# Second expert stage: weights per block from DRAM into a ring, in place of a resident copy

## The chip, the cores and the metric

The kernel runs on one core of one Trainium2 chip. The metric is the device time of the program in microseconds, of which several runs are taken. The engines are PE (matrix products), DVE, ACT and POOL (elementwise work; POOL also starts indirect DMAs) and SP (which only starts DMAs). Each has its own stream of instructions; they meet through semaphores.

## What is computed

The input x has 128 graphs of 64 nodes with 128 features, 8192 tokens in all. Four parts follow each other, each adding to x what it makes of the normalised x:

```python
x = x + gated_graph(layernorm(x), adj)      # 3 GRU layers
x = x + experts_1(layernorm(x))             # 8 experts, top 2, relu
x = x + relational(layernorm(x), adj)       # 40 relations, two directions
x = x + experts_2(layernorm(x))             # 8 experts, top 2, gelu
```

The last of them, which the change is about, computes all experts for all tokens and takes two per token:

```python
top_p, top_idx = jax.lax.top_k(probs, 2)
weights = top_p / top_p.sum(axis=-1, keepdims=True)
xe = xn[None, :, :] * ln_g[:, None, :] + ln_b[:, None, :]
h = gelu(jnp.einsum('end,edh->enh', xe, W1) + b1[:, None, :])   # h: 512 wide
y = jnp.einsum('enh,ehd->end', h, W2) + b2[:, None, :]
```

The kernel computes only the two chosen experts of each token.

## The kernel before

**Stages.** The program runs setup, first_norm, gated_graph, experts "1", relational, experts "2" and combine one behind the other; a barrier of all engines stands between them. The function `experts` is used twice, with m = 0 for the first and m = 1 for the second. In the trace the tiles of the second have names that begin with e2, those of the first with e1.

**Routing and blocks.** Each token is sent twice, once for each of its experts, from the tile ROWS in SBUF into a DRAM array `slots`, where the rows of one expert stand together. These sends are POOL's indirect DMAs (L570), 256 in a stage; most are issued in the stage before, and the last 32 at the start and in the first iterations of the expert stage, four per iteration. The slots are worked off in 39 blocks of 512 rows. A block belongs to one expert, which depends on the data: a table `owner` gives it, `start_row` the block's first row. Eight "tail" DMAs (L1259, one per expert, in the iterations b = 3 to 10) fill up the last rows of each expert.

**One block.** SP loads the block's rows transposed into xT (L1246 reads the row number from the table, L1247 is the DMA) and its labels (L1253). PE computes the up product, 4 chunks of 128 hidden rows with 3 matmuls each (the weights are kept as a high and a low f16 half, L358 to L360). ACT applies the bias and the activation (L1356, L1361), DVE splits the result (L1374). PE opens the output with the b2 rows (L1317, 2 matmuls) and computes the down product with 32 matmuls (L1323, L1325). DVE weighs and sums the two halves (L1409, L1411, L1415), and POOL scatters the 512 rows to `results` with 4 indirect DMAs (L1293). PE's order is the up product of block b+1, then the down product of block b. All buffers are rings of three (RING = 3). Blocks 0 to 2 and 33 to 38 are written out, blocks 3 to 32 run in a hardware loop of 5 turns of 6 blocks (L59, L1234).

**Where the weights are.** W1 and W2 in SBUF hold both halves of all 8 experts, 2 MB each. Since the owner of a block is data, PE reads it into a register (L1304, once before the up and once before the down product) and addresses the weights with it:

```python
def who(b):
    return pe.value_load(owner[0:1, bass.ds(b, 1)], min_val=0, max_val=E - 1)
passes(pe, HB[c][:, :], lambda s: W1[:, s, bass.ds(e * HID + c * P, P)],
       lambda s: xT[j][:, s, :], True, True).then_inc(h_ps, 1)
```

The second stage's weights are prepared during gated_graph and written to two DRAM arrays, kept[0] and kept[1]. At the start of the relational stage, when the first experts are through, SP loads both back into W1 and W2 (L1558 to L1560), ahead of its other DMAs. Those are four row loads (L1562) and the tiles c_G (L1433), the expert results which DVE adds to X (L1426). At its end SP waits for the two reloads. In combine the results are loaded as d_G by the same line.

## Time and profile before

| | us |
|---|---|
| median of 3 runs | 1657.19 |
| the runs | 1643.72, 1657.19, 1658.66 |
| the profiled execution's own time | 1653.87 |
| its span | 1652.1 |
| experts "1" (from its first xT load) | 604 to 946 |
| relational | 946 to 1267 |
| experts "2", first matmul to last scatter | 1279 to 1605 |
| combine, first load to the end | 1609 to 1652 |

The profile is of one execution. Its rows give a start in us from the span's start, a duration in us, the engine, the line of the kernel and the operation, out<-in by tile names. "q" behind an engine's name (SPq) marks its sequencer, which issues DMAs. In brackets stands how long the engine had been idle and what released it: "issue" means that nothing the profile shows was being waited for, and "remote" that it was a semaphore from another engine whose last visible operation had long ended. PE matmul rows overlap, since the ends are modelled.

### The profile page before, as it was taken

Reading aid. Unit: us, or ns where it says so; the run is one execution under the profiler, and the core shown is the slowest. Engines: PE = TensorE matmul, PEld = TensorE weight load, DVE = VectorE, ACT = ScalarE, POOL = GpSimd, SP = SyncE. Lnnn points to the kernel's source line nnn. Section 1 sums busy time; section 2 is a strip of 40 time slices with the busy share of each in tenths; the row PEclk is TensorE's granted clock in tenths of the full one; section 3 lists DMA queues with packets and bytes.
Section 4 is the critical chain, followed back from the end, with each engine's and each line's share of the span. In section 5 each row is a group of like instructions: output and inputs, shape, how many; then the busy total and the mean of one; then the engine's idle time right before and its main releaser. Section 6 shows DMA issues by size and latency. Waiting matters only on the chain. (4 is left out here: it accounts for less than half of the span.)

```text
span 1652.1 us, 23983 instructions
## 1 busy us (share of the span) xinstructions
PE 970.9 (59%) x6685; PEld 540.3 (33%) x6686; DVE 993.0 (60%) x2486; ACT 745.7 (45%) x1300; POOL 777.8 (47%) x751
## 2 busy tenths in 40 slices
PE   2046758676850625678898334545440767898850
PEld 1023324333330512345554212322220424455530
DVE  5957778878784333456666425565662444676645
ACT  0135556464541533456665324544540534666630
POOL 2322324757546005665666501156665366565650
PEclk8569989898875556889999755555555778999985
DMA  7010010202105342433333141021101334333309
GB/s 191 0 26 1 20 32 24 56 28 62 40 21 161 128 115 66 97 79 73 71 64 70 30 146 39 27 66 60 47 33 51 78 81 93 74 74 65 79 10 304
DMA packets 234271, 114.92 MB, mean 70 GB/s; under 512 B 172816, under 2 KB 218002, under 8 KB 233656
## 3 DMA queue, kind: packets, MB, share of 16 engines
q1 hardware_dynamic: 203400, 69.07, 18.3%
q0 software_dynamic: 18176, 34.14, 6.5%
q10 hardware_dynamic: 12592, 10.49, 2.3%
q8 instruction: 45, 0.74, 0.2%
q14 instruction: 58, 0.48, 0.1%
HBM read 41.76 MB, written 51.08 MB: 56 GB/s over the span
## 5 line engine op out<-in xcount | busy, mean ns | idle before, releaser
L570 POOL DMA_INDIRECT slots<-ROWS,pos x256 | 269.8, 1054 | 159.1 <-POOLq L152 86.3
L1293 POOL DMA_INDIRECT results<-e1ys,e1home x156 | 167.3, 1072 | 129.2 <-DVE e1ys L1415 82.8
L1293 POOL DMA_INDIRECT results<-e2ys,e2home x156 | 169.6, 1087 | 121.1 <-DVE e2ys L1415 75.4
L1356 ACT ACTIVATE e1hf<-psum,VT 128x512 f32<-128x512 f32 x156 | 104.3, 687 | 149.8 <-remote 76.9
L1356 ACT ACTIVATE e2hf<-psum,VT 128x512 f32<-128x512 f32 x156 | 104.1, 688 | 131.6 <-remote 84.4
L1176 POOL TENSOR_TENSOR a_gates<-a_gates,a_state 128x512 f32<-128x512 f32 x48 | 62.8, 1308 | 166.8 <-ACT a_gates L923 165.9
L1323 PE MATMUL psum<-W,e1hs 128*128 x624 | 120.5, 286 | 25.0 <-issue 21.1
L1323 PE MATMUL psum<-W,e2hs 128*128 x624 | 121.5, 285 | 22.7 <-issue 20.2
L1374 DVE SCALAR_TENSOR_TENSOR e1hs<-e1hf,e1hs 128x512 f16<-128x512 f32 x156 | 101.8, 690 | 42.8 <-ACT e1hs L1361 35.7
L1325 PE MATMUL psum<-W,e2hs 128*128 x624 | 114.9, 227 | 16.5 <-issue 16.3
L1325 PE MATMUL psum<-W,e1hs 128*128 x624 | 114.3, 227 | 16.6 <-issue 16.5
L1374 DVE SCALAR_TENSOR_TENSOR e2hs<-e2hf,e2hs 128x512 f16<-128x512 f32 x156 | 101.1, 688 | 36.5 <-ACT e2hs L1361 27.1
L1545 POOL TENSOR_TENSOR c_rs<-c_var,mhalf 128x12 f32<-128x12 f32 (+2 forms) x19 | 37.8, 1990 | 151.8 <-DVE c_var L1802 119.4
L1361 ACT ACTIVATE e2hs<-e2hf 128x512 f16<-128x512 f32 x156 | 94.3, 635 | 0.0
L1361 ACT ACTIVATE e1hs<-e1hf 128x512 f16<-128x512 f32 x156 | 94.2, 634 | 0.0
L358 PE MATMUL psum<-e1xT,W 128*128 128x512 f16 x156 | 61.9, 396 | 40.3 <-DMA e1xT<-slots 31.7
L1409 DVE TENSOR_SCALAR e2both<-psum 128x512 f32<-128x512 f32 x39 | 26.8, 688 | 97.5 <-remote 97.2
L1409 DVE TENSOR_SCALAR e1both<-psum 128x512 f32<-128x512 f32 x39 | 26.8, 688 | 91.9 <-remote 91.2
L1323 PEld LDWEIGHTS psum<-W,e2hs 128*128 128x128 f16 x624 | 63.1, 101 | 49.4 <-issue 41.3
L358 PE MATMUL psum<-a_state,WHH 128*128 128x512 f16 x144 | 59.0, 410 | 34.3 <-DMA a_state<-ROWS 27.1
L1323 PEld LDWEIGHTS psum<-W,e1hs 128*128 128x128 f16 x624 | 63.1, 101 | 46.3 <-issue 37.9
L935 ACT ACTIVATE a_state<-a_state 128x512 f16<-128x512 f32 x48 | 30.2, 629 | 103.8 <-DVE a_state L1032 97.0
(345 smaller groups left out, 2720.5 us busy)
## 6 DMA issues: line engine op xcount, KB each, us to landing
c_G<-results SPq DMA_DIRECT2D x32, 256.0 KB, 3.2
d_G<-results SPq DMA_DIRECT2D x32, 256.0 KB, 6.0
slots<-slots SPq DMA_DIRECT2D x16, 264.0 KB
slots<-ROWS,pos POOLq DMA_INDIRECT x256
kept<-a_norm SPq DMA_DIRECT2D x4, 1024.0 KB, 4.3
W<-kept SPq DMA_DIRECT2D x2, 2048.0 KB, 10.0
out_dram<-X ACTq DMA_DIRECT2D x16, 256.0 KB, 5.9
results<-e1ys,e1home POOLq DMA_INDIRECT x156
```

Source lines behind the costliest of these rows:

```text
L358: pe.matmul(out, lhs(0), rhs(0), start=start, stop=False, skip_group_check=True)
L570: pool.indirect_dma_start(out=slots, out_offset=bass.IndirectOffsetOnAxis(ap=k["pos"][:, c, t:t + 1], axis=0), in_=k["ROWS32"][:, t, :], i ...
L935: act.activation(hT[p][:, 0, :], H[p][:, :], ACT.Copy).then_inc(h_hi, 1)
L1176: pool.tensor_tensor(Z[p % 2][:, :], Z[p % 2][:, :], H[p][:, :], ALU.mult).then_inc(zh_sb, 1)
L1293: pool.indirect_dma_start(out=k["results"][m], out_offset=bass.IndirectOffsetOnAxis(ap=home[:, GT * b + q:GT * b + q + 1], axis=0), in_=ys ...
L1323: pe.matmul(YB[v][:, q // 2, :, q % 2, :], hs[j][:, 0, c, q * P:(q + 1) * P], W2[:, 0:2, w2], start=False, stop=False, skip_group_check=True)
L1325: t = pe.matmul(YB[v][:, q // 2, 0, q % 2, :], hs[j][:, 1, c, q * P:(q + 1) * P], W2[:, 0, w2], start=False, stop=c == CH - 1, skip_group_ ...
L1356: act.activation(hf[c][:, :], HB[c][:, :], func, bias=VT[:, bass.ds(e * CH + b1_col + c, 1)], scale=1 / PS).then_inc(h_f32, 1)
L1361: act.activation(hs[j][:, 0, c, :], hf[c][:, :], ACT.Copy, scale=AS).then_inc(h_hi, 1)
L1374: dve.scalar_tensor_tensor(out=hs[j][:, 1, c, :], in0=hf[c][:, :], scalar=AS, in1=hs[j][:, 0, c, :], op0=ALU.mult, op1=ALU.subtract).then_ ...
L1409: dve.tensor_scalar(whole, YB[v][:, :, 0, :, :], 1 / PS, None, ALU.mult).then_inc(y_half, 1)
L1545: pool.tensor_tensor(rstd[s % 4][:, lo:hi], var[s % 2][:, lo:hi], k["mhalf"][:, lo:hi], ALU.pow)\
```

## The change

In the second expert stage (staged is true for m = 1) the weights aren't resident. SP has a new function `weights(b, w)`: it reads the owner of block b and starts a DMA of that expert's W1 (w = 0) or W2 (w = 1), 128 x 2 x 512 f16 = 256 KB in pieces of 1 KB, from kept[w] into slot b % 3 of a ring that lies in the old W1 tile, and a semaphore for each slot and w counts them. Six loads stand at the start of the stage, ahead of SP's wait for the sends. In iteration b, W1 of block b+3 follows the xT load of block b+3, and W2 of block b+2 follows that block's labels, behind a wait until the down product of block b-1 is done (y_ps >= b). PE waits for w_in[0] ahead of the up product and for w_in[1] ahead of the down product; its up and down matmuls have fixed addresses, and who(b) is called once a block, for the b2 rows. The two reloads in the relational stage and the wait for them are gone. The first expert stage computes as before, from the resident tiles.

```diff
--- before.py
+++ after.py
@@ -1222,6 +1222,9 @@
             sem(n) for n in ("h_ps", "h_f32", "h_hi", "h_lo", "y_ps", "y_half", "y_sum", "y_sb"))
         counted, listed, tails, match, weight, homes = (
             sem(n) for n in ("counted", "listed", "tails", "match", "weight", "homes"))
+        staged = m == 1
+        held = W1[:, :, :].rearrange("p s n -> p (s n)")[:, 0:4 * RING * HID].rearrange("p (j w s n) -> p j w s n", j=RING, w=2, s=2)
+        w_in = [[sem(f"w{w}_in{j}") for j in ring] for w in range(2)]
         HB = banks[0:4]
         YB = [k["psum"][:, 4 + 2 * j:6 + 2 * j, :].rearrange("p b (h q d) -> p b h q d", h=2, q=2) for j in range(2)]
         both = [sb(f"both{j}", [P, GT, P], F32) for j in range(2)]
@@ -1258,6 +1261,16 @@
                 row = sp.value_load(end_row[0:1, e:e + 1], min_val=0, max_val=k["DUMP"])
                 sp.dma_start(slots[bass.ds(row, BLK), :], slots[k["DUMP"]:k["DUMP"] + BLK, :]).then_inc(tails, 16)
 
+            def weights(b, w):
+                e = sp.value_load(owner[0:1, b:b + 1], min_val=0, max_val=E - 1)
+                sp.dma_start(held[:, b % RING, w, :, :],
+                             k["kept"][w].rearrange("p (s n) -> p s n", s=2)[:, :, bass.ds(e * HID, HID)])\
+                    .then_inc(w_in[w][b % RING], 16)
+
+            if staged:
+                for b in ring:
+                    for w in range(2):
+                        weights(b, w)
             sp.wait_ge(sent[0], 16 * N_EARLY)
             rows = {}
             for b in ring:
@@ -1275,8 +1288,13 @@
                 if b + RING < NBLK:
                     sp.wait_ge(h_ps, 4 * b + 4)
                     rows[b + RING] = load(b + RING)
+                    if staged:
+                        weights(b + RING, 0)
                 if 1 <= b and b + 2 < NBLK:
                     read_tags(b + 2, rows.pop(b + 2))
+                    if staged:
+                        sp.wait_ge(y_ps, b)
+                        weights(b + 2, 1)
 
         @block.gpsimd
         def _(pool):
@@ -1306,8 +1324,11 @@
             def up_c(b, j, e, i, c):
                 if c == 0:
                     pe.wait_ge(x_loaded[j], 16 * (i + 1))
+                    if staged:
+                        pe.wait_ge(w_in[0][j], 16 * (i + 1))
                 wait_from(pe, h_f32, 4 * b + c - 3)
-                passes(pe, HB[c][:, :], lambda s: W1[:, s, bass.ds(e * HID + c * P, P)],
+                passes(pe, HB[c][:, :], lambda s: held[:, j, 0, s, c * P:(c + 1) * P] if staged
+                       else W1[:, s, bass.ds(e * HID + c * P, P)],
                        lambda s: xT[j][:, s, :], True, True).then_inc(h_ps, 1)
 
             def open_y(b, j, v, e):
@@ -1319,26 +1340,28 @@
 
             def down_q(b, j, v, e, q):
                 for c in range(CH):
-                    w2 = bass.ds(e * HID + c * P, P)
-                    pe.matmul(YB[v][:, q // 2, :, q % 2, :], hs[j][:, 0, c, q * P:(q + 1) * P], W2[:, 0:2, w2],
+                    w2 = held[:, j, 1, :, c * P:(c + 1) * P] if staged else W2[:, 0:2, bass.ds(e * HID + c * P, P)]
+                    pe.matmul(YB[v][:, q // 2, :, q % 2, :], hs[j][:, 0, c, q * P:(q + 1) * P], w2,
                               start=False, stop=False, skip_group_check=True)
-                    t = pe.matmul(YB[v][:, q // 2, 0, q % 2, :], hs[j][:, 1, c, q * P:(q + 1) * P], W2[:, 0, w2],
+                    t = pe.matmul(YB[v][:, q // 2, 0, q % 2, :], hs[j][:, 1, c, q * P:(q + 1) * P], w2[:, 0, :],
                                   start=False, stop=c == CH - 1, skip_group_check=True)
                 return t
 
-            e = who(0)
+            e = None if staged else who(0)
             for c in range(CH):
                 up_c(0, 0, e, 0, c)
 
             def step(b, j, i, v):
                 if not last(b):
                     j1, i1 = (j + 1) % RING, i + (j + 1) // RING
-                    e = who(b + 1)
+                    e = None if staged else who(b + 1)
                     for c in range(CH):
                         up_c(b + 1, j1, e, i1, c)
                 e = who(b)
                 open_y(b, j, v, e)
                 pe.wait_ge(h_lo, 4 * b + 4)
+                if staged:
+                    pe.wait_ge(w_in[1][j], 16 * (i + 1))
                 for q in range(GT):
                     t = down_q(b, j, v, e, q)
                 t.then_inc(y_ps, 1)
@@ -1484,7 +1507,6 @@
         T = BATCH * GT
         Q = Route(nc, ctx, k, "v", T)
         B = Blocks(nc, ctx, k, "v")
-        back = sem("weights_back")
 
         AC, AT = sb("AC", [P, GT, P], F16), sb("AT", [P, GT, P], F16)
         HG = sb("HG", [P, GT, 2, 2, P], F32)
@@ -1556,8 +1578,6 @@
 
         @block.sync
         def _(sp):
-            for n, w in enumerate((k["W1"], k["W2"])):
-                sp.dma_start(w[:, :, :].rearrange("p s n -> p (s n)"), k["kept"][n]).then_inc(back, 16)
             for n, name in enumerate(("b_fwd", "bg_fwd", "b_bwd", "bg_bwd")):
                 sp.dma_start(relrows[:, n * P:(n + 1) * P], ins["L1_gnn_" + name]).then_inc(rows_packed, 16)
             for g in two:
@@ -1573,7 +1593,6 @@
                         sp.dma_start(BB[:, :, :, :].rearrange("p a b c -> p (a b c)"),
                                      relrows[bass.ds(r, 1), :].to_broadcast([P, 4 * P])).then_inc(g_bias, 16)
                     turns(sp, RELS, rel)
-            sp.wait_ge(back, 32)
 
         @block.tensor
         def _(pe):
```

On PE, in the second expert stage, between the up product of block 0 and the down product of block 0 (e2xT1 is the input of block 1, W1 the weights; TENSOR_LOAD is a table read, ISA is register arithmetic, an address or an assertion). The up product of block 1 before:

```order
L1304 TENSOR_LOAD owner
L1304 ISA x2
L358 ISA
L358 MATMUL psum<-e2xT1,W1 128x512
L359 MATMUL psum<-e2xT1,W1 128x512
L360 ISA
L360 MATMUL psum<-e2xT1,W1 128x512
L358 ISA
```

and the same place after:

```order
L358 MATMUL psum<-e2xT1,W1 128x512
L359 MATMUL psum<-e2xT1,W1 128x512
L360 MATMUL psum<-e2xT1,W1 128x512
L358 MATMUL psum<-e2xT1,W1 128x512
L359 MATMUL psum<-e2xT1,W1 128x512
L360 MATMUL psum<-e2xT1,W1 128x512
```

The table read and an address instruction ahead of each group of matmuls are gone. On PE, a little further on, at the start of block 0's down product (e2hs0 is its hidden layer), before:

```order
L1304 TENSOR_LOAD owner
L1304 ISA x2
L1317 ISA
L1317 MATMUL psum<-b2rows,ones16 128x256 x2
L1323 ISA
L1323 MATMUL psum<-W2,e2hs0 128x2x128
L1325 MATMUL psum<-W2,e2hs0 128x128
L1323 ISA
```

and after:

```order
L1322 TENSOR_LOAD owner
L1322 ISA x2
L1338 ISA
L1338 MATMUL psum<-b2rows,ones16 128x256 x2
L1344 MATMUL psum<-W1,e2hs0 128x2x128
L1346 MATMUL psum<-W1,e2hs0 128x128
```

The read of the owner stays, since the b2 rows need it; the address instructions ahead of L1323 are gone (there are four), and the weights now come from the W1 tile, in which the ring lies.

On SP, in the second expert stage, the load for the fourth or fifth block and its labels, before:

```order
L1246 TENSOR_LOAD start_row
L1246 ISA x2
L1247 ISA
L1247 DMA_TRANSPOSE e2xT1<-slots1 128x2x512
L1253 ISA
L1253 DMA e2label<-slots1 128x4x4
```

and after (W1 here is the ring, kept0 and kept1 the DRAM arrays):

```order
L1250 ISA
L1250 DMA_TRANSPOSE e2xT1<-slots1 128x2x512
L1265 TENSOR_LOAD owner
L1265 ISA x2
L1266 ISA
L1266 DMA W1<-kept0 128x2x512
L1256 ISA
L1256 DMA e2label<-slots1 128x4x4
L1265 TENSOR_LOAD owner
L1265 ISA x2
L1266 ISA
L1266 DMA W1<-kept1 128x2x512
```

Each xT load is followed by a table read and a load of 256 KB, and each label by another such pair.

## Rows read from the trace of the kernel before

**Rows 1.** Busy by stretches: window, its us, each engine's busy us, PEclk, DMA share, GB/s.

```profile
1279.00:1302.00 23.00, 22.67 (x153) 13.09 (x154) 16.48 (x36) 19.22 (x33) 5.15 (x5) 0.88 0.54 89
1302.00:1387.00 85.00, 51.40 (x276) 24.89 (x275) 27.28 (x49) 25.80 (x46) 53.12 (x53) 0.70 0.33 81
1387.00:1555.00 168.00, 148.46 (x1107) 87.66 (x1105) 114.77 (x201) 108.95 (x195) 105.59 (x96) 0.97 0.34 74
```

**Rows 2.** Timeline of PE, 1292 to 1301: start us, us, operation.

```profile
1292.86 0.39 PE L1317 MATMUL psum<-b2rows,ones 2*128 x2
...
1298.52 0.39 PE L1317 MATMUL psum<-b2rows,ones 2*128 x2
```

**Rows 3.** L1317's matmuls in 1387:1555 and 1279:1594: ns, first and last start.

```profile
L1317 PE MATMUL psum<-b2rows,ones x48: 267/272/389, 1389.5 to 1551.3; 2*128 x48
L1317 PE MATMUL psum<-b2rows,ones x78: 264/275/412, 1287.0 to 1589.1; 2*128 x78
```

**Rows 4.** Timeline of PE, 1306 to 1322: [idle before <- what ended it].

```profile
1313.29 0.37 PE L1323 MATMUL psum<-W,e2hs 128*128 x1 [1.59 <-issue]
...
1319.25 0.42 PE L1323 MATMUL psum<-W,e2hs 128*128 x1
```

**Rows 5.** DVE's group of L1409, 1279 to 1594: busy us, mean ns, idle before.

```profile
L1409 DVE TENSOR_SCALAR e2both<-psum 128x512 f32<-128x512 f32 x38 | 26.2, 688 | 93.1 <-remote 92.9 <-PE psum L1325 0.3
```

**Rows 6.** Timeline of POOL from 1290, then its scatters of 1279 to 1610.

```profile
1295.64 1.29 POOL L1293 DMA_INDIRECT results<-e2ys,e2home  x1 [17.28 <-DVE e2ys L1415]
...
1315.53 0.96 POOL L570 DMA_INDIRECT slots<-ROWS,pos  x1 [0.30 <-issue]
L1293 POOL DMA_INDIRECT results<-e2ys,e2home x156 | 169.6, 1087 | 121.1 <-DVE e2ys L1415 75.4 <-issue 45.7
```

**Rows 7.** Timelines of POOL, PE, DVE at the relational stage's end.

```profile
1258.39 0.96 POOL L570 DMA_INDIRECT slots<-ROWS,pos  x1 [0.30 <-issue]
1245.92 0.45 PE L546 MATMUL psum<-v_both,ones 128*128 128x64 f16 x8
1250.33 0.19 DVE L1861 TENSOR_TENSOR S<-psum,c_rs 128x32 f32<-128x32 f32 x1 [5.50 <-remote]
```

**Rows 8.** The DMA queues in 1390 to 1550: packets, MB, share of 16 engines.

```profile
q14 instruction: 3, 0.02, 0.1%
```

**Rows 9.** Timelines of SP and DVE where relational and where combine starts.

```profile
946.28 0.83 SPq L1560 DMA_DIRECT2D W<-kept  x2
...
950.67 42.92 SPq L1433 DMA_DIRECT2D c_G<-results  x12
960.83 1.42 DVE L1426 TENSOR_TENSOR X<-X,c_G 128x512 f32<-128x512 f32 x2 [13.33 <-DMA c_G<-results]
1609.37 2.81 SPq L1433 DMA_DIRECT2D d_G<-results  x3
1614.05 1.42 DVE L1426 TENSOR_TENSOR X<-X,d_G 128x512 f32<-128x512 f32 x2 [14.57 <-DMA d_G<-results]
```

**Rows 10.** Timeline of SP, 1350 to 1364; then L1253's DMAs in 1302:1594, ns.

```profile
1353.04 0.70 SPq L1253 DMA_DIRECT2D e2label<-slots  x1
1355.91 0.88 SPq L1259 DMA_DIRECT2D slots<-slots  x1
...
1362.18 0.41 SPq L1253 DMA_DIRECT2D e2label<-slots  x1
1363.38 0.57 SPq L1259 DMA_DIRECT2D slots<-slots  x1
L1253 SPq DMA_DIRECT2D e2label<-slots x33: 17/429/749, 1322.1 to 1568.3; - x33
```

**Rows 11.** Timelines of SP and PE at the second expert stage's start.

```profile
1275.30 1.34 SPq L1247 DMA_TRANSPOSE e2xT<-slots  x1
...
1278.05 1.30 SPq L1247 DMA_TRANSPOSE e2xT<-slots  x1
1279.19 0.61 PE L358 MATMUL psum<-e2xT,W 128*128 128x512 f16 x1 [16.17 <-DMA e2xT<-slots]
```

## Prediction: what it does to the time

> **What bounds the kernel now.** The change touches the start of the relational stage and the second expert stage. I read the latter by stretches first, then PE's, DVE's and POOL's rows, then SP's.
>
> The table by stretches shows PE busy 22.67 of 23 us while blocks 0 to 2 run, but 51.40 of 85 in the loop's first turn (blocks 3 to 8) and 148.46 of 168 in its four later turns [rows 1]. No other engine comes near: PE is the stage's engine, with holes.
>
> How large are the holes? Without one a block costs 5.66 us, the distance of the b2 matmuls (L1317) of blocks 1 and 2, 1292.86 to 1298.52 [rows 2]. Each block has two of them, and the 78 start from 1287.0 to 1589.1, 38 periods of 7.95 us [rows 3]. So (7.95 - 5.66) x 38 = 87 us of the stage are holes. From block 2 at 1298.5 to block 9 at 1389.5 stand 7 x 5.66 = 39.6 us of work in 91.0, a loss of 51; from there to block 32 (1551.3) 23 x 5.66 = 130.2 in 161.8, a loss of 32; the rest is 4 [rows 2, 3].
>
> What are they? Not waits for data. In the down product PE stops again and again (1.59 us ahead of 1313.29) with "<-issue", nothing awaited that the profile shows, until at 1319.25 it runs on [rows 4]. DVE is held up behind it: 92.9 us of its idle time in the stage go to "remote", ahead of the first reading of the down product's result [rows 5]. What happens meanwhile is that POOL issues indirect DMAs without a pause, 16 in a row from 1295.64 to 1316.5 [rows 6]; PE's crawl ends 2.8 us behind that burst. While POOL was silent, until 1295.64, PE went through blocks 0 to 2, register-addressed as well, with no hole [rows 1, 6].
>
> **The change, part by part.**
>
> 1. *PE's instructions.* Before, each block has two reads of the owner table and an address computation ahead of nearly every weight slice; after, one read, and up and down matmuls have fixed addresses. Counting matmuls, their weight loads and the rest, the order gives PE some 111 instructions a block before and 96 after: 15 fewer, 13.5%. Where PE doesn't crawl this is worth nothing, since it is busy for 22.67 of 23 us there [rows 1]: the small instructions already hide behind running matmuls, and the floor of 5.66 us stays. Where it crawls, two bounds. If every instruction costs alike in a crawl, 13.5% of 87 = 12 us go. If POOL's burst alone sets how long the crawl lasts, it is nothing. For the second speaks that code without any register address shows the same lateness: under the 20 sends that end the relational stage, the last at 1258.39, PE's small matmuls are on record by 1246.4, and DVE gets the result of those ahead of them only at 1250.33, after 5.50 us of "remote" [rows 7]. I take the middle, **-6**, since one end has a count and the other a row for it.
>
> By the Trainium skill, "Runtime: NRT & Kernel Launch", section "Instruction fetch mechanics", instructions come in blocks of 16 KiB, prefetch is sequential, and a taken branch outside the window forces a fetch; by that rule the holes are fetch stalls that shrink with the code, and the term would be -12. The trace disagrees: in 1390 to 1550, with some 32 us of holes, q14 brought three packets, 0.02 MB [rows 8].
>
> 2. *The reload taken out of the relational stage.* Two DMAs of 2 MB stand first on SP there (946.28), then four row loads, and c_G, which the stage's first DVE work needs, at 950.67; DVE has it at 960.83, 10.2 us later [rows 9]. With nothing ahead the same load (d_G in combine) is issued at 1609.37 and used at 1614.05, 4.7 us later [rows 9]. After the change c_G is issued the 0.85 us of two issues earlier, at 949.8, and used at 954.5: **-6.3**. Lower bound 0, if later waits took it up; since the whole stage starts behind this wait, I take it whole. SP's closing wait for the reload goes too, at nothing: it was satisfied some 300 us before.
>
> 3. *Six weight loads ahead of the stage.* SP enters the stage when the relational stage ends (1267) and waits for the sends; its first transpose is at 1275.30, the first matmul at 1279.19 [rows 11]. Into that time go six pairs of a table read and a DMA. None exists in the trace; the nearest is a tail copy, from the end of the label at 1362.59 to 1363.95, 1.36 us, and in a crawl 1353.74 to 1356.79, 3.05 us [rows 10]. 6 x 1.36 = 8.2 brings SP from 1267.8 to 1276.0, about 1.4 us past the point where it now starts, and the feed chain moves with it: **+1.4**. In a crawl, 18.3 us: +11.4. SP's own transposes there stand at the normal 2.75 us, under POOL's sends, so I take the low end.
>
> 4. *Two weight loads per block.* SP's work per block is a load of xT and a label, first transpose to second: 2.75 us [rows 11]. Two more pairs of 1.36 make it 5.5, plus 1.36 in the eight iterations with a tail. That is below the mean block (7.95) and just below the floor (5.66). W1's part is issued once the up product three blocks before is done, W2's once the down product two blocks before it has begun; each has two blocks and more, some 14 us at the floor, and 256 KB are there 4.7 us after issue (d_G) [rows 9]. So neither is late: **0**. Behind SP's new wait for y_ps stands the next xT load; that wait is for the end of a down product, 2.8 us behind the up product that SP waited for already, and xT has the same 14 us.
>
> 5. *Traffic.* 78 x 256 KB = 20 MB, 512 KB per block. The reload's 4.2 MB and c_G were through in 14.5 us (946.28 to 960.83) [rows 9], so 512 KB fill the DMA engines for 1.8 us at most, and the share of 0.34 [rows 1] rises to some 0.57. I take **0**: the stretch with a share of 0.54 is the one without holes, and the densest holes stand at 0.33 [rows 1]. Against it speaks the Trainium skill, "DMA: Bandwidth & Descriptors", section "Issuing engines are not separate DMA queues": what SP, ACT and POOL start runs on the same 16 engines and interleaves. The late c_G is this case's row for it; by that rule the 20 MB hold up scatters and transposes too.
>
> Sum on the profiled execution: 1653.9 - 6.3 + 1.4 - 6 = 1643.0. The median of the runs is 3.3 above that execution's own time, so **1646**.
>
> **Rivals.**
>
> *A: the holes come from the register addresses and vanish, faster.* For it: they are marked "issue", and the mean block is 40% over the floor. Against it: blocks 0 to 2, and the lateness in static code [rows 1, 7]. Then 87 us would be free, but POOL becomes the bound: 156 scatters at 1.09 + 0.30 and 28 sends at 0.96 + 0.30 [rows 6] are 252 us; begun at 1295.6 they end at 1548 instead of 1605.5, -58. Own 1653.9 - 6.3 + 1.4 - 58 = 1591, median **1594**.
>
> *B: SP becomes the bound, slower.* In a crawl SP's work costs 3.05 / 1.36 = 2.24 times as much [rows 10]: 12.3 us a block against 7.95. If it crawled for the 63% of the time that POOL is busy in the later turns [rows 1], its mean would be 5.5 + 0.63 x 6.8 = 9.8, and 39 x (9.8 - 7.95) = +72. Own 1653.9 - 6.3 + 1.4 + 72 = 1721, median **1724**. It decides once SP crawls for over 36% of the time, (7.95 - 5.5) / 6.8. Against it: over the loop the median label issue is 429 ns, next to 0.41 us in the undisturbed row [rows 10].
>
> *C: the traffic stretches the holes, slower.* If they grew with the DMA share, 0.34 to 0.57, 87 us become 146: +59, median **1711**; contention in a third of the stage gives +20, median 1672. Against it are the shares just named.
>
> That the change doesn't do what it says is excluded by the order: the address instructions are gone from PE, and the loads stand on SP.
>
> **How the numbers follow.** The forecast 0.50, with a range of its own of 1636 to 1660 (holes -12 to 0, reload -6.3 to 0, start +1.4 to +8). A 0.27, B 0.11, C 0.07, and 0.05 for small mishaps within 1%. One per cent, 16.6 us (1640.6 and 1673.8), is about what a measurement of this kernel can tell from no change, its three runs being 15 us apart. Of the forecast's 0.50, 0.12 lie below 1640.6 (the whole of the 12 us) and 0.38 within. Faster 0.27 + 0.12 = 0.39; same 0.38 + 0.05 = 0.43; slower 0.11 + 0.07 = 0.18. The range runs from A's 1594 less one to 1676, where B and most of C (0.15) and the lowest bit of A are left out.
>
> **What would show it.** Step 1: L1317's pairs 7.8 us apart on average, 5.66 in blocks 0 to 2, "issue" holes still under POOL's bursts, and near 87 us of "remote" ahead of L1409's successor; A is right if they are under 6.7 us apart and POOL runs without idle time. Step 2: DVE's first c_G work at 954 to 955. Step 3: the second expert stage's first matmul at 1279.2 - 6.3 + 1.4 = 1274.3. Step 4: hardly a wait of PE for the ring; if "DMA W" ends much of its idle time, B or C. Wrong altogether would be the idea that POOL's bursts set the holes, if PE runs on through a burst once its addresses are fixed.

## The result, and the profile after

The changed kernel is slower by a little: 1665.63 us median of 20 runs (1653.5 to 1674.78) against 1653.51 of 20 runs of the kernel before (1643.72 to 1668.63) on the same chip. The ratio is 1.0067, 95% interval 1.0046 to 1.0089. In two later jobs it was 1.0044 (1.0019 to 1.0070) and 1.0051 (1.0021 to 1.0082). I had forecast 1646, 0.7% below the 1657.19 that was known then. The time is inside my range of 1593 to 1676 and within 1% of no change, but on the other side.

The profiled execution took 1667.73 us (span 1665.9). The table by stretches of the second expert stage (window, its us, each engine's busy us, PEclk, DMA share, GB/s) answers to [rows 1]:

```profile
1273.00:1296.00 23.00, 22.58 (x152) 12.97 (x153) 16.25 (x36) 19.26 (x33) 4.91 (x5) 0.87 0.66 127
1296.00:1382.00 86.00, 49.97 (x275) 25.94 (x274) 29.21 (x51) 27.33 (x48) 53.46 (x54) 0.72 0.48 118
1382.00:1565.00 183.00, 154.44 (x1109) 90.55 (x1109) 112.46 (x197) 105.90 (x187) 103.92 (x96) 0.92 0.57 137
1565.00:1604.00 39.00, 34.11 (x262) 20.49 (x260) 28.32 (x50) 25.41 (x46) 24.21 (x24) 0.96 0.41 92
```

The first stretch is as full as before (22.58 of 23), the first turn as empty (49.97 of 86). The third row begins some 10 us ahead of block 9 and [rows 1] only 2.5, so their lengths, 183 and 168 us, don't compare. From block 9's b2 matmuls to block 33's, 24 blocks in both, it is 175.9 us where it was 167.9: PE is idle for 24.8 in place of 19.5, and busy for 151.1 in place of 148.4 at a granted clock of 0.94 in place of 0.97. So most of the 8 us are holes, and some 2.7 are longer matmul time, beside the lower clock. The DMA share rose from 0.34 to 0.57, as worked out. The b2 matmuls of all 39 blocks, min/median/max ns, first and last start:

```profile
L1338 PE MATMUL psum<-b2rows,ones x78: 264/276/406, 1281.5 to 1599.8; 2*128 x78
```

From 1281.5 to 1599.8 are 38 periods of 8.38 us, against 7.95 in [rows 3] and the forecast 7.8. The holes look as in [rows 4]; the timeline of PE under POOL's first burst, and of DVE at its end:

```profile
1307.08 0.37 PE L1344 MATMUL psum<-W,e2hs 128*128 128x256 f16 x1 [1.74 <-issue]
...
1310.58 0.37 PE L1344 MATMUL psum<-W,e2hs 128*128 128x256 f16 x1 [1.13 <-issue]
...
1313.37 0.27 PE L1346 MATMUL psum<-W,e2hs 128*128 128x128 f16 x1 [1.02 <-issue]
1313.47 0.69 DVE L1432 TENSOR_SCALAR e2both<-psum 128x512 f32<-128x512 f32 x1 [16.96 <-remote]
```

PE stops for 0.93 to 1.74 us ahead of single matmuls, though their addresses are fixed now. The first two groups of DVE and POOL that answer to [rows 5, 6]:

```profile
L1432 DVE TENSOR_SCALAR e2both<-psum 128x512 f32<-128x512 f32 x38 | 26.1, 688 | 97.9 <-remote 95.6 <-PE psum L1346 2.3
L1311 POOL DMA_INDIRECT results<-e2ys,e2home x156 | 167.7, 1075 | 146.4 <-DVE e2ys L1438 102.0 <-issue 44.4
```

"Remote" ahead of DVE's reading of the down product is 95.6 us, against 92.9. The relational start, SP and DVE, answers to [rows 9]:

```profile
947.63 36.86 SPq L1456 DMA_DIRECT2D c_G<-results  x12
951.74 1.42 DVE L1449 TENSOR_TENSOR X<-X,c_G 128x512 f32<-128x512 f32 x2 [6.44 <-DMA c_G<-results]
```

c_G is used 4.1 us after its issue (10.2 before), and 7.6 us after DVE's work ahead of it (a copy at 944.14), where that was 14.5 (946.33 to 960.83): 6.9 us less. The start of the second expert stage, POOL's first send, SP's six weight loads and first transpose, PE's first matmul, answers to [rows 11]:

```profile
1259.57 0.96 POOL L570 DMA_INDIRECT slots<-ROWS,pos  x1 [9.25 <-POOLq L152]
1259.63 7.76 SPq L1266 DMA_DIRECT2D W<-kept  x6
1268.35 1.10 SPq L1250 DMA_TRANSPOSE e2xT<-slots  x1
1273.42 0.61 PE L358 MATMUL psum<-e2xT,W 128*128 128x512 f16 x1 [19.38 <-DMA e2xT<-slots]
```

The kernel before has its first send there at

```profile
1268.55 0.96 POOL L570 DMA_INDIRECT slots<-ROWS,pos  x1 [9.20 <-POOLq L152]
```

so it is 10.6 us from the first send to the first matmul before (1279.19) and 13.9 after: +3.2 us.

Last, what SP waits for in the stage (us in total, times, longest), after and then before:

```profile
SPq L1265 <- remote: 52.0, 16, 8.5
SPq L1249 <- remote: 10.8, 4, 6.7
SPq L1249 <- PE psum L360: 6.2, 3, 2.9
```

```profile
SPq L1246 <- remote: 105.1, 12, 19.9
SPq L1246 <- PE psum L360: 46.3, 18, 6.7
SPq L1276 <- remote: 7.1, 1, 7.1
SPq L1253 <- DVE e2share L1391: 4.5, 4, 1.4
```

SP has lost more than half of its waiting time (69 us in place of 163), but it has some left, so it isn't the bound.

### The profile page after: what moved, and what is told of

Its sections match the earlier page's. It is cut to its first block and busy times, and to the rows that moved or that the text cites. A ratio compares the mean times of both kernels' runs of the same rounds, so it can differ in the third digit from the quotient of the medians.

```text
span 1665.9 us, 23929 instructions
## 1 busy us (share of the span) xinstructions
PE 980.2 (59%) x6685; PEld 546.6 (33%) x6686; DVE 993.0 (60%) x2486; ACT 747.1 (45%) x1300; POOL 776.1 (47%) x751
## 5 line engine op out<-in xcount | busy, mean ns | idle before, releaser
L1344 PE MATMUL psum<-W,e2hs 128*128 128x256 f16 x624 | 119.5, 285 | 26.1 <-issue 24.5
L1344 PE MATMUL psum<-W,e1hs 128*128 x624 | 120.2, 286 | 18.6 <-issue 16.4
L1346 PE MATMUL psum<-W,e2hs 128*128 128x128 f16 x624 | 114.3, 227 | 12.7 <-issue 12.6
L358 PE MATMUL psum<-e2xT,W 128*128 128x512 f16 x156 | 65.4, 419 | 28.2 <-DMA e2xT<-slots 19.4
```

The lines of the kernel that those rows point to most:

```text
L358: pe.matmul(out, lhs(0), rhs(0), start=start, stop=False, skip_group_check=True)
L1344: pe.matmul(YB[v][:, q // 2, :, q % 2, :], hs[j][:, 0, c, q * P:(q + 1) * P], w2, start=False, stop=False, skip_group_check=True)
L1346: t = pe.matmul(YB[v][:, q // 2, 0, q % 2, :], hs[j][:, 1, c, q * P:(q + 1) * P], w2[:, 0, :], start=False, stop=c == CH - 1, skip_group_c ...
```

## The experiments

Eighteen runs of nine kernels were made, in five jobs, each beside the kernel before. Each job has a chip of its own, and the chips are of two kinds. On some the kernel before takes 1653 to 1672 us and PE crawls, as in the recorded profile: it stops for a microsecond or so ahead of single matmuls while POOL issues indirect DMAs. On others it takes 1532 and PE doesn't crawl. No chip came twice in the five jobs, so the chip and the moment aren't parted. All comparisons are ratios to the kernel before in the same job, with 95% intervals in brackets; of them only the plain DMA's differ by more than 2%. The edits are shown shortened.

| kernel | chips where PE crawls | where it doesn't |
|---|---|---|
| the kernel before | 1653.5, 1653.3, 1671.5, 1672.0 us | 1532.3, 1531.9 us |
| changed kernel | 1.0067, 1.0044, 1.0051 | not run |
| before, reload later | 0.9961 (0.9938 to 0.9985) | not run |
| changed, no loads in the loop | 0.9933 (0.9904 to 0.9962) | 0.9968, 0.9971 |
| changed, 32-byte rows | 1.0031 (1.0004 to 1.0059) | 0.9942, 0.9975 |
| changed, one partition only | 1.0100 (1.0062 to 1.0138) | not run |
| changed, loads from a fixed address | 0.9986 (0.9959 to 1.0013) | not run |
| changed, PE's addresses from registers | 1.0109 (1.0064 to 1.0153) | 0.9962, 0.9985 |
| before, plain DMA for the scatters | 0.9395 (0.9339 to 0.9450) | 0.9701, 0.9754 |

### First job: the parts one by one

**e1_noloads** leaves the loads inside the loop and SP's wait for y_ps out; all blocks use the weights of blocks 0 to 2. PE's wait for w_in[1] is changed as the one for w_in[0] is.

```diff
-                        weights(b + RING, 0)
-                        sp.wait_ge(y_ps, b)
-                        weights(b + 2, 1)
-                        pe.wait_ge(w_in[0][j], 16 * (i + 1))
+                        pe.wait_ge(w_in[0][j], 16)
```

> The changed kernel without the 72 weight loads inside the block loop (only the six ahead of the stage remain; PE's waits for the ring ask for the first load only, SP's new wait for y_ps is gone). All blocks use the weights of blocks 0 to 2, so this leaves out the right weights and keeps PE's fixed addresses. Theory T (the 20 MB of traffic stretch PE's crawl under POOL's bursts): the stage loses what it gained in length, 16 us or more, and keeps the 6.9 us of the relational start: about 1643 where the kernel before is at 1653 (0.99 or less), L1338-pairs 7.8 us apart. Theory S (SP's own added instructions are what costs): the same number. Theory P (fixed addresses themselves give nothing or cost): 8.3 us apart as in the changed kernel, ratio 1.005 or more. If fixed addresses remove the crawl, which the traffic then brought back: under 7 us apart, 1610 or less.

**e2_tiny** cuts each load's rows from 1 KB to 32 bytes, so most of the weights aren't loaded.

```diff
-                sp.dma_start(held[:, b % RING, w, :, :],
-                    ...[:, :, bass.ds(e * HID, HID)])
+                sp.dma_start(held[:, b % RING, w, :, 0:16],
+                    ...[:, :, bass.ds(e * HID, 16)])
```

> The changed kernel with each of its 78 weight loads cut from 1 KB to 32 bytes a row: the same instructions on SP, the same number of packets, 1/32 of the bytes; the weights are mostly not those of the block's expert. Theory T by bytes: as without loads, about 1643, ratio 0.99. Theory S, or T by packets: as the changed kernel, ratio 1.006, pairs of b2 matmuls 8.3 us apart.

**e3_dyn** puts PE's register addresses back, and the second read of the owner with them: both products read the resident W2 tile, so the up product has other weights, while all loads and waits stay. The up product's edit:

```diff
-                       held[:, j, 0, s, c * P:(c + 1) * P] if staged
+                       (W2 if staged else W1)[:, s, bass.ds(e * HID + c * P, P)]
```

> The changed kernel with PE's register addresses put back: both products read the resident W2 tile at the owner's address (so the up product uses the wrong weights), all loads and waits of the change stay. It parts the loads from the addresses. If fixed addresses are worth the 12 us that my upper bound gave, this is 12 us slower than the changed kernel, 1677 (ratio 1.014). If they are worth nothing, it is equal to it, ratio 1.0067. Under theory P it is faster than the changed kernel, ratio near 1.0.

**e4_plain** is the kernel before with one plain DMA to fixed rows in place of a block's four indirect scatters, in the second expert stage alone, so the results aren't in their tokens' rows; the 28 sends stay. The number of POOL's DMAs falls with it, and that isn't parted from their kind.

```diff
-                for q in range(GT):
-                    pool.indirect_dma_start(out=k["results"][m], ...)
+                pool.dma_start(k["results"][m][r:r + BLK, :].rearrange("(q p) d -> p q d", p=P),
+                               ys[b % RING][:, :].rearrange("p (q d) -> p q d", q=GT))
```

> The kernel before, with the 4 indirect scatters of each block in the second expert stage replaced by one plain DMA from POOL to fixed rows (the results are then in the wrong order; the 28 sends stay). If POOL's bursts of indirect DMAs are what holds PE up, the holes vanish but for the first turn's sends: b2 pairs near 6 us apart and the stage 60 us or more shorter, 1590 (ratio 0.96). If the register addresses or code fetching make the holes, the pairs stay 7.95 us apart, and only the last block's scatters (5 to 15 us at the end) are saved, ratio 0.99 to 0.995.

The kernel before took 1532.31 us in this job, 7% less than in the recorded one, and no expectation had allowed for such a chip. In the order above the ratios were 0.9968 (0.9938 to 0.9999), 0.9942 (0.9917 to 0.9967), 0.9962 (0.9934 to 0.9990) and 0.9701 (0.9653 to 0.9749). The groups of POOL and DVE and the b2 matmuls of e1_noloads, second expert stage:

```profile
L1306 POOL DMA_INDIRECT results<-e2ys,e2home x156 | 171.4, 1099 | 67.8 <-issue 47.3 <-DVE e2ys L1433 20.5
L1427 DVE TENSOR_SCALAR e2both<-psum 128x512 f32<-128x512 f32 x39 | 26.9, 690 | 60.0 <-DMA results<-e2ys,e2home 58.0 <-issue 2.1
L1333 PE MATMUL psum<-b2rows,ones x78: 267/272/278, 1220.9 to 1463.2; 2*128 x78
```

POOL's 156 scatters stand with 0.30 us between them, hardly a wait for DVE (20.5 us, the first one's), and DVE waits 58.0 us for buffers that POOL has still to store. There is no "remote". The blocks are 6.38 us apart. POOL is the bound here as in my rival A, and it is so with the chip. It isn't reached by fixed addresses: e3_dyn has register addresses, and its blocks are 6.43 us apart. The first expert stage, which is the same code in all these kernels and has register addresses, shows it too. Its b2 matmuls in the kernel before (recorded profile), and then in e1_noloads:

```profile
L1317 PE MATMUL psum<-b2rows,ones x78: 264/276/416, 615.4 to 921.7; 2*128 x78
L1333 PE MATMUL psum<-b2rows,ones x78: 267/272/278, 612.7 to 857.1; 2*128 x78
```

Periods of 8.06 and 6.43 us: one code, two chips. Some 1.6 us for each of 38 periods in two expert stages make 122 us, about the whole distance of 1653.5 to 1532.3.

### Second job: the changed kernel, before, and the reload moved

> The changed kernel itself once more, with the kernel before on the same chip, since the last four kernels ran on a chip where the kernel before takes 1532 us and PE shows no crawl under POOL's indirect DMAs. If this is a chip of that kind: POOL bounds the block loop, so only the relational start (-6.9) and the stage's start (+1 to +3) count, ratio 0.996 to 0.998. If it is a chip of the first kind (the kernel before at 1653): 1.0067 again.

> The kernel before itself, for a profile on the same chip. If the chip is of the second kind, POOL's 184 DMAs of the second expert stage stand without a gap and b2 pairs are 6.4 us apart, which would show that the holes of the recorded profile come with the chip and not with the code. If of the first kind, pairs are 7.9 us apart as recorded.

**e5_reload_late** is the kernel before with the two reloads behind the first four loads of c_G:

```diff
-            for n, w in enumerate((k["W1"], k["W2"])):
-                sp.dma_start(w[:, :, :]..., k["kept"][n]).then_inc(back, 16)
             ...
             for g in two:
                 fetch(sp, k, 0, g, G[g], gathered[g])
+            sp.wait_ge(gathered[1], 32)
+            for n, w in enumerate((k["W1"], k["W2"])):
+                sp.dma_start(w[:, :, :]..., k["kept"][n]).then_inc(back, 16)
```

> The kernel before with the two reloads of 2 MB moved behind the first four c_G loads of the relational stage, so that they no longer delay the first of them; all else of before stays. If the change's gain is the reload alone: DVE's first c_G work 6.9 us earlier, ratio 0.9955 to 0.9965 on either kind of chip. If the late c_G costs elsewhere (the next c_G waits for the reload in its turn): about 1.0.

This chip is of the kind on which PE crawls, the kernel before at 1653.33. The changed kernel came to 1.0044. The b2 matmuls of the kernel before, in one more execution:

```profile
L1317 PE MATMUL psum<-b2rows,ones x78: 264/276/416, 1282.8 to 1592.1; 2*128 x78
```

That is 38 periods of 8.14 us, 0.19 more than in the recorded profile of the same kernel; so much a period of a single trace may vary. e5_reload_late gave 1645.28 us, ratio 0.9961, -6.4 us. Its SP and DVE at the relational start:

```profile
942.59 2.16 SPq L1433 DMA_DIRECT2D c_G<-results  x4
948.83 0.81 SPq L1565 DMA_DIRECT2D W<-kept  x2
946.60 1.42 DVE L1426 TENSOR_TENSOR X<-X,c_G 128x512 f32<-128x512 f32 x2 [6.35 <-DMA c_G<-results]
```

The first c_G is used 4.0 us after its issue, and behind this wait of 6.35 us the profile names no further one of DVE's c_G additions for a DMA, so the 4 MB delay nothing that shows. This version is 0.4% faster than the kernel before (0.15 to 0.6%) and 0.8 to 1.1% faster than the changed one.

### Third job: the separating kernels once more

> The kernel of e1_noloads again (fixed addresses on PE, no weight load inside the block loop, wrong weights), for a chip of the first kind, where PE crawls under POOL's indirect DMAs and the changed kernel is 1.0044 to 1.0067 of the kernel before. Theory T (traffic stretches the crawl): ratio 0.99 or less. Theory P (fixed addresses give nothing or cost): 1.004 or more. Between them (0.996, the reload's gain alone): fixed addresses are worth nothing, and the loads cost the 13 to 17 us.

> The kernel of e2_tiny again (all 78 loads and their waits, but 32 bytes a row in place of 1 KB), for a chip of the first kind. If the bytes are the cost: as without loads. If SP's instructions, its wait or the number of packets are the cost: as the changed kernel, 1.0044 to 1.0067.

> The kernel of e3_dyn again (all loads and waits of the change, but PE reads the resident W2 tile at the owner's address in both products), for a chip of the first kind. Fixed addresses worth 12 us: ratio 1.012 to 1.014. Worth nothing: as the changed kernel, 1.0044 to 1.0067. Theory P: under 1.0.

> The kernel of e4_plain again (the kernel before with one plain DMA from POOL in place of each block's four indirect scatters), for a chip of the first kind. If POOL's indirect DMAs hold PE up: b2 pairs near 6 us apart, ratio 0.96 or less (1590). If not: pairs 7.9 us apart, 0.99 to 0.995. On a chip of the second kind it was 0.970, since POOL was the bound there.

Another chip without the crawl (kernel before 1531.91): 0.9971, 0.9975, 0.9985, 0.9754. It repeats the first job and says nothing about the crawl. On both such chips all three changed kernels are 0.2 to 0.6% faster than before (e3_dyn_b's interval, 0.9952 to 1.0018, holds no change too), about the reload's 6.4 us of 1532 (0.4%). The changed kernel itself wasn't run there.

### Fourth job: the same on a chip that crawls

> The kernel without the loads inside the block loop (fixed addresses, wrong weights), on whichever chip comes. Where the kernel before takes 1653 (PE crawls): if the loads' traffic is what made the change slower, ratio 0.996 or less; if fixed addresses save 12 us as well, 0.989; if neither, 1.004 or more. Where it takes 1532 (no crawl): 0.997 as twice before.

> All loads of the change, but PE's register addresses kept (resident W2 tile for both products). Where PE crawls: 1.0044 to 1.0067 as the changed kernel if fixed addresses are worth nothing, 1.012 if they are worth 12 us, below 1.0 if they cost. Where it doesn't: 0.996 to 0.999.

> All 78 loads at 32 bytes a row. Where PE crawls: if bytes are the cost, as e1_noloads_c; if SP's instructions, its new wait or the packets are, 1.0044 to 1.0067. Where it doesn't: 0.994 to 0.998.

> The changed kernel once more beside the three above. Where PE crawls: 1.0044 to 1.0067. Where it doesn't (1532): POOL is the bound of the block loop, only the reload's 6.4 us less the stage start's 2 count, 0.997.

The kernel before took 1671.51 us. Of the b2 matmuls of e1_noloads_c, after_again_c and e3_dyn_c, first and last start:

```profile
L1333 PE MATMUL psum<-b2rows,ones x78: 264/275/416, 1291.5 to 1603.0; 2*128 x78
```

```profile
L1338 PE MATMUL psum<-b2rows,ones x78: 264/277/416, 1279.1 to 1602.6; 2*128 x78
```

```profile
L1337 PE MATMUL psum<-b2rows,ones x78: 264/277/416, 1293.6 to 1623.2; 2*128 x78
```

Periods of 8.20, 8.51 and 8.67 us, and ratios of 0.9933, 1.0051 and 1.0109. Two differences follow, in this job's us. The loads inside the loop, with the wait that came with them, cost 1.0051 - 0.9933 = 1.18%, 19.7 us; the runs' means lie 19.9 us apart, give or take 4. Fixed addresses save 1.0109 - 1.0051 = 0.58%, 9.7 us; the means lie 9.5 apart, give or take 5. So they are worth something, and theory P falls. With rows of 32 bytes the kernel is at 1.0031, 0.20% or 3.3 us from the full loads, inside the noise and just below the 1.0044 expected, and 17.5 us (give or take 4) above the kernel without loads: the bytes aren't what costs, though the loads do.

### Fifth job: instructions or packets, and POOL's part

**e6_onerow** loads one partition, 2 rows of 32 bytes (the source is cut in the same way):

```diff
-                sp.dma_start(held[:, b % RING, w, :, :],
+                sp.dma_start(held[0:1, b % RING, w, :, 0:16],
```

> The changed kernel with each weight load cut to one partition and 32 bytes a row: all of SP's instructions, table reads and waits stay, but 2 packets in place of 256 (and no weights to speak of). Where PE crawls: if SP's instructions are the cost, as e2_tiny_c and the changed kernel, 1.003 to 1.006; if the packets are (writing or moving their descriptors), as without loads, 0.993 to 0.996. Where it doesn't crawl: 0.995 to 0.998.

**e7_fixed** drops the table read and the address, so that all loads bring the first expert's weights, in full:

```diff
-                e = sp.value_load(owner[0:1, b:b + 1], min_val=0, max_val=E - 1)
-                    ...[:, :, bass.ds(e * HID, HID)])
+                    ...[:, :, 0:HID])
```

> The changed kernel with the loads in full, but always from the first expert's weights, so SP needs one instruction per load instead of five (no table read, no assertion, no address; wrong weights). Where PE crawls: if SP's instructions are the cost, 0.993 to 0.996, as without loads; if the transfers and packets are, 1.004 to 1.006. Where it doesn't crawl: 0.995 to 0.998.

> The kernel before with one plain DMA from POOL per block in place of the four indirect scatters. Where PE crawls: if POOL's indirect DMAs are what it crawls under, holes remain only in the first turn (28 sends): b2 pairs near 6.2 us apart, ratio 0.96 or less; if not, 0.99. Where it doesn't: 0.970 to 0.975, as twice before.

The kernel before took 1672.01 us. With hardly a packet left, e6_onerow is no faster, 1.0100, above the 1.003 to 1.006 expected; with all packets but one SP instruction per load in place of five, e7_fixed is at 0.9986, between the 0.993 to 0.996 and the 1.004 to 1.006 that the two theories gave. The b2 matmuls of the two:

```profile
L1338 PE MATMUL psum<-b2rows,ones x78: 267/278/416, 1295.2 to 1622.9; 2*128 x78
```

```profile
L1337 PE MATMUL psum<-b2rows,ones x78: 264/275/387, 1280.0 to 1591.4; 2*128 x78
```

8.62 and 8.19 us apart. And that the transfers of e6_onerow are really gone shows in its queues in 1390 to 1550, against those of the changed kernel behind them and e7_fixed's, last, whose loads run on the same queue as before (packets, MB, share):

```profile
q1 hardware_dynamic: 31649, 5.89, 22.1%
q14 instruction: 4, 0.03, 0.1%
```

```profile
q1 hardware_dynamic: 44711, 16.96, 47.8%
q14 instruction: 5, 0.04, 0.1%
```

```profile
q1 hardware_dynamic: 46828, 17.49, 48.4%
```

So packets and bytes are not the cost, and SP's instructions are: from 1.0051 to 0.9986 the four further instructions of each load are worth 0.65%, 10.9 us. That is across two jobs, since the changed kernel didn't run in the fifth, and the two intervals give it an uncertainty of 7 us; 1.3 us of it lie at the stage's start, where e7_fixed needs 12.6 us from the first send to the first matmul and the changed kernel 13.9. Within the fifth job e6_onerow and e7_fixed are 18.6 us apart, give or take 5. That is more than the four instructions, for e6_onerow's own are longer: its table reads take 446 ns in the median and its issues 662, where the changed kernel's take 278 and 554. From e7_fixed to no loads at all (0.9933) 0.53%, 8.9 us, again across two jobs and with an uncertainty of 7, stay for the DMA instruction itself and the wait for y_ps; these weren't parted.

e4_plain_c gave 0.9395, 1570.6 us. POOL's plain DMAs, DVE's first reading of the down product, the b2 matmuls, and two stretches of the stage:

```profile
L1294 POOL DMA_DIRECT2D results<-e2ys x39 | 29.7, 761 | 172.6 <-DVE e2ys L1420 162.6 <-issue 10.0
L1414 DVE TENSOR_SCALAR e2both<-psum 128x512 f32<-128x512 f32 x39 | 26.7, 685 | 12.3 <-remote 11.4 <-PE psum L1330 0.9
L1322 PE MATMUL psum<-b2rows,ones x78: 264/268/278, 1297.9 to 1522.1; 2*128 x78
```

```profile
1295.00:1350.00 55.00, 48.20 (x370) 29.10 (x369) 38.37 (x75) 35.56 (x65) 29.79 (x30) 1.00 0.55 129
1350.00:1500.00 150.00, 148.54 (x1200) 95.03 (x1199) 127.49 (x223) 121.30 (x214) 24.27 (x31) 1.00 0.47 101
```

"Remote" falls from 92.9 to 11.4 us, the blocks are 5.90 us apart, and PE is busy for 148.54 of 150 us once the 28 sends are over. The crawl of PE, on the chips that have it, is due to POOL's indirect DMAs, four of them a block.

How does an instruction of SP slow a stage in which SP has time to spare? Its loads don't come late. In the changed kernel's trace I took, for each block from the fourth on, the time from the end of the issue to PE's first matmul that needs the data: at least 9.4 us for xT, 8.1 for W1 and 9.0 for W2, medians 14.4, 12.7 and 14.0. This holds the transfer too, but none of PE's waits in the stage, in any of the three traces of this kernel, is put down to a weight load. While PE crawls, SP crawls too. The durations of SP's three register instructions per load (ns, min/median/max) in the changed kernel, and then in e3_dyn on a chip without the crawl:

```profile
L1265 SPq TENSOR_LOAD <-owner x72: 15/278/524, 1280.7 to 1590.0; - x72
L1265 SPq FUSED_REGOPS  x72: 4/157/712, 1281.0 to 1590.3; - x72
L1265 SPq SEQ_ASSERT  x72: 3/18/701, 1281.2 to 1590.5; - x72
```

```profile
L1265 SPq TENSOR_LOAD <-owner x69: 267/279/547, 1230.0 to 1454.5; - x69
L1265 SPq FUSED_REGOPS  x69: 152/157/164, 1230.3 to 1454.8; - x69
L1265 SPq SEQ_ASSERT  x69: 18/18/26, 1230.5 to 1455.1; - x69
```

The medians are the same, 278, 157 and 18 ns, but single ones of the latter two take 0.7 us, where they never take over 0.17 on the other chip. Of SP's rows between the first b2 matmul and the last, 62 of 760 in the changed kernel start 0.6 to 0.8 us behind a row that isn't a DMA; in the kernel before 11 of 334, in e7_fixed 12 of 405, in e3_dyn on the other chip 1 of 760. And where SP has more of them, PE has fewer: in the first turn, from 8 us into each of POOL's bursts to its end, the records show SP's rows at 1.04 to 1.08 per us in three traces of the changed kernel (0.33 to 0.41 in three with before's loop), and PE's at 2.0 to 2.3 (2.7 to 4.2), register instructions counted; matmuls and weight loads alone are at 1.6 to 1.8 (2.1 to 3.4). Where the addresses are fixed and SP has less to do, e7_fixed has 0.15 and 3.1, e1_noloads_c 0.07 and 3.2. The two add up to 3.1 to 3.4 rows per us in all of these but the kernel before's recorded trace (4.5); in e3_dyn_c they come to 2.7. These are counts in single traces, but they go one way: as if the sequencers took turns at something that POOL's indirect DMAs keep busy. What that is, the runs don't show.

## Why the prediction was wrong

The step that failed is step 4, the loads inside the loop, put at 0 and measured at +19.7 us. Term by term, forecast and then measured, in us of this kernel:

| term | forecast | measured |
|---|---|---|
| reload taken out | -6.3 | -6.4 (e5_reload_late) |
| stage start, six loads | +1.4 | +3.2 (the two traces) |
| PE's fixed addresses | -6 (0 to -12) | -9.7 (changed less e3_dyn_c) |
| loads inside the loop: SP's part and traffic (steps 4 and 5) | 0 | +19.7 (changed less e1_noloads_c) |
| sum | -10.9 | +6.8 |

The change as measured is +7 to +12 us, so the terms hold together. That the time lies inside my range is luck: I had opened the range upwards for SP as the bound or for traffic, and neither came.

- **The bound** was read rightly as far as it went: PE with holes under POOL's bursts. e4_plain_c shows that the bursts cause them. I had taken it from coincidence in time, from blocks 0 to 2 and from the static code of the relational stage [rows 6, 7], and all three pointed right. What I couldn't see is that they do so on some chips only.
- **Step 1** was nearer its upper bound. If every instruction costs alike in a crawl, 15 of 111 give 12; the runs give 9.7, give or take 5. The halving between "count" and "nothing" had no ground in a mechanism: that POOL causes the crawl doesn't mean that the instruction count in it is free.
- **Step 2** came out: -6.4 as a ratio (0.9938 to 0.9985, so -2 to -10), and -6.9 in the traces. DVE's c_G work came at 951.7, not 954.5, partly since the stage began 2.2 us earlier than in the trace before.
- **Step 3** was 1.8 us short. SP's part was near: its first transpose stands 8.8 us behind the first send, where it was 6.8. The other 1.2 us lie between that transpose and the first matmul, 5.07 us in place of 3.89 (5.1 and 5.5 in the two later traces). They are the bytes of the six loads just issued: from the end of the transpose's issue to the matmul it is 4.0 us, but 2.6 before, 2.7 in e2_tiny_c with rows of 32 bytes, and 2.6 in e7_fixed, whose full loads end 5.4 us ahead of the transpose. The first matmul came at 1273.4 where 1274.3 was forecast only because the stages ahead had ended earlier.
- **Step 4 is the step that failed.** "So neither is late: 0." That was true, and it did not follow. I priced SP's loads by whether SP keeps up and the data land in time, and both hold (69 us of SP's waits left, no wait of PE for a weight load). But I had a crawl in which each instruction of PE was said to cost time, and I had seen SP crawl in it too [rows 10]; I took away 15 instructions of PE there and didn't ask what putting 10 of SP's there, two of them DMAs, would do. The order gave their number. Priced as PE's were, at 12 us for 15 a block, ten more are +8, and with -12 in step 1 the sum is still a gain of 9 us; so the count alone wouldn't have given the sign. By the runs SP's ten cost 19.7 us and PE's fifteen 9.7, some three times as much each. The row that hinted at it is the pair of a table read and a DMA that took 3.05 us in a crawl in place of 1.36 [rows 10]: I used it for rival B, as SP's own time, and never as a price that PE might pay.
- **Step 4, a slip of wording**: W2 of block b+2 is issued once the down product of block b-1 is done, three blocks before, not two. The 14 us stand.
- **Step 5** held inside the loop: 0 for the bytes. The DMA share went to 0.57, and neither 32-byte rows nor 2 packets a load made it faster beyond the noise. At the stage's start the bytes cost the 1.2 us told under step 3.
- **Rival B** had the right engine and the wrong mechanism. SP was to become the bound from a crawl of over 36% of the time; it never was. **Rival C** fell with step 5. **Rival A**, no crawl and POOL the bound, is real, but the change doesn't bring it about: it is how the other chips run the variants, with register addresses or without.
- **The rule on instruction fetch** (Trainium skill, "Runtime: NRT & Kernel Launch", section "Instruction fetch mechanics") gave -12 for step 1, and the 9.7 measured lies between that and my -6, too roughly to choose. The cause that it names the trace still doesn't show: q14 brought 5 packets, 0.04 MB, in 160 us of the changed kernel's loop.
- **A sum of mine** was wrong: the forecast's own range of 1636 to 1660 doesn't follow from its bounds. -12, -6.3 and +1.4 give 1640, and 0, 0 and +8 give 1665.
- **What the range lacked**: no case joined a true gain on PE with a cost of the same kind on SP, and I had put only 0.05 on small mishaps. The outcome, within 1%, had 0.43.

## What to carry to other kernels

While GpSimd (POOL) issues indirect DMAs back to back, look whether other engines' instructions come in steps of some 0.7 us. Where they did so here, instructions on PE and on SP both cost time, although SP had time to spare. Moving work from one sequencer to another didn't pay even though the number of instructions fell by five a block: 15 fewer on PE gained 10 us and 10 more on SP, two of them DMAs, cost 20. A large load that stands ahead of the stage's first small one is worth moving by itself: that alone saved 6.4 us, and it needs no ring.

## What the runs showed of the hardware that was not expected

- The same program takes 1653 to 1672 us on some chips and 1532 on others, 8 to 9% apart. The first expert stage's blocks are 8.06 us apart in the recorded profile and 6.43 in e1_noloads, with one code. A change may be worth something on one kind and nothing on the other, so a job's ratio holds for its chip.
- On chips with the crawl, four indirect DMAs of POOL per block in place of one plain one cost 6% of the whole kernel (0.9395); on those without, 2.5 to 3% (0.9701 and 0.9754), and there because POOL itself is the bound.
- A register instruction of SP that takes 157 ns takes up to 712 ns in a crawl, and single partition loads of 2 packets cost the stage no less than loads of 256 KB (1.0100 and 1.0051).
- Six loads of 256 KB issued just ahead of a transposing DMA held it up by some 1.4 us; with 32 bytes a row they didn't.
